# The second layer's messages by units of two chunks, on VectorE alone, in a four-layer graph kernel

## The reference, cut to what matters

```
es = ys[dst]; ev = yv[dst]
m0a = wA * es * sh0
m0b = wD * jnp.einsum('eud,ed->eu', ev, sh1) * INV_SQRT3
m1a = wB[:, :, None] * es[:, :, None] * sh1[:, None, :]
m1b = wC[:, :, None] * ev * sh0[:, :, None]
mid_s = jnp.concatenate([m0a, m0b], axis=1)
mid_v = jnp.concatenate([m1a, m1b], axis=1)
ns = jax.ops.segment_sum(mid_s, src, num_segments=N)
nv = jax.ops.segment_sum(mid_v, src, num_segments=N)
```

## Time and profile before

| | |
|---|---|
| median of 3 runs | 10667.19 us |
| profiled execution | 10687.69 us, span 10685.9 us, mean granted TensorE clock 0.813 |
| DVE busy over the span | 5953.1 us (56%) |
| POOL busy over the span | 5768.1 us (54%) |
| PE busy over the span | 6312.3 us (59%) |
| third stage, first product of DVE to last addition | 5806.15 to 7104.76 us |

### The profile page before, as it was taken

One profiled execution on the slowest core, in us unless ns is written; L12 is line 12 of the kernel. 1 busy time (PEld: TensorE's weight loads), 2 busy tenths in 40 slices (PEclk: granted clock), 3 DMA queues, 4 the chain that ended last, 5 costly groups with the idle time before them and its releaser, 6 DMA issues. The chain is left out here.

```text
span 10685.9 us, 108870 instructions
## 1 busy us (share of the span) xinstructions
PE 6312.3 (59%) x23693; PEld 3434.3 (32%) x23693; DVE 5953.1 (56%) x17820; ACT 2842.7 (27%) x9327; POOL 5768.1 (54%) x6086
## 2 busy tenths in 40 slices
PE   2211344446865666666667777765555578856665
PEld 1101233334433333433334111233333333333332
DVE  8915533430016666544445999976656589943333
ACT  0000000105862222100003777762222236500000
POOL 5776566561006666566662888844555510046664
PEclk9999855558987877888887999996666679978877
DMA  2000111113553333433332555534666645523333
GB/s 79 6 6 5 36 42 46 44 33 124 176 194 96 93 93 93 109 91 91 91 90 67 168 171 169 171 91 141 189 184 186 185 128 176 153 80 91 92 91 82
DMA packets 782920, 1136.72 MB, mean 106 GB/s; under 512 B 161213, under 2 KB 631923, under 8 KB 775629
## 3 DMA queue, kind: packets, MB, share of 16 engines
q0 software_dynamic: 246400, 552.44, 19.6%
q1 hardware_dynamic: 535885, 577.31, 16.6%
HBM read 872.21 MB, written 257.00 MB: 106 GB/s over the span
## 5 line engine op out<-in xcount | busy, mean ns | idle before, releaser
L1155 POOL DMA_INDIRECT ring<-scaled_table,idx_s x832 | 787.2, 946 | 1181.1 <-DVEq L192 773.7
L1029 POOL DMA_INDIRECT big<-x_table,rec_d_sb x808 | 806.1, 998 | 1101.1 <-DMA x_table<-big 726.0
L1748 POOL DMA_INDIRECT ring<-att_table,rec_d_sb x808 | 775.6, 960 | 750.7 <-DVE acc L1858 287.6
L1427 PE MATMUL bank<-ring,wts 128*128 128x512 f32 x1664 | 937.6, 648 | 397.2 <-issue 166.7
L1105 PE MATMUL bank<-iota 128*128 128x512 bf16 x2448 | 1090.0, 445 | 0.0
L333 POOL DMA_INDIRECT rec_s<-acc,big x784 | 837.6, 1068 | 375.0 <-issue 253.7
L1349 POOL DMA_INDIRECT ring<-y_table,idx_s x832 | 815.2, 980 | 395.5 <-DVEq L192 171.3
L333 POOL DMA_INDIRECT rec_d<-x_res,big x784 | 750.5, 957 | 502.0 <-DVE big L596 255.5
L1155 POOL DMA_INDIRECT ring<-h_table,rec_d_sb x808 | 764.1, 946 | 470.6 <-issue 180.4
L1116 PE MATMUL bank<-big,ring 128*128 128x256 f32 x1616 | 620.5, 473 | 501.0 <-issue 363.7
L2088 PE MATMUL bank<-ring 128*128 128x256 f32 x1664 | 644.9, 475 | 421.0 <-DVE ring L2070 244.4
(11 more groups left out here) (344 smaller groups left out, 13324.4 us busy)
## 6 DMA issues: line engine op xcount, KB each, us to landing
weights_dram<-acc SPq DMA_DIRECT2D x104, 1024.0 KB, 4.5
ring<-weights_dram SPq DMA_DIRECT2D x832, 128.0 KB
rows_spill<-ring SPq DMA_DIRECT2D x808, 128.0 KB
big<-rows_spill SPq DMA_DIRECT2D x808, 128.0 KB, 2.2
ring<-key_dram SPq DMA_DIRECT2D x49, 1024.0 KB
big<-dl_dram SPq DMA_DIRECT2D x50, 512.0 KB
ring<-y_table,idx_s POOLq DMA_INDIRECT x832
ring<-scaled_table,idx_s POOLq DMA_INDIRECT x832
```

Source lines behind the costliest of these rows:

```text
L1029: g.indirect_dma_start(out=xg[:, c % RG, :], out_offset=None, in_=x_table, in_offset=bass.IndirectOffsetOnAxis(ap=recd3i[:, c, D_IDX:D_IDX ...
L1155: g.indirect_dma_start(out=slot[:, c % ring_len, :], out_offset=None, in_=table, in_offset=bass.IndirectOffsetOnAxis(ap=index(c), axis=0)) ...
L1427: pe.matmul(ps[6 + u % 2], oh1[c // 4 % 2][:, c % 4, :], mid[:, c % 2, 0:512], start=(c % GS == 0), stop=(c % GS == GS - 1)).then_inc(summ ...
L1748: g.indirect_dma_start(out=ag[:, n % R3, :], out_offset=None, in_=att_table, in_offset=bass.IndirectOffsetOnAxis(ap=recd3i[:, n, D_IDX:D_I ...
```

## The change

DVE's loop goes over units. One instruction takes both chunks of a unit: the reduction (L1391 of the new code), the A and B products together (L1396), the C product (L1399), and, for the unit before, the D product (L1407) and the product with the harmonics (L1410). Then comes the addition (L1420), now of the unit six back (before, a unit was added one chunk after its last product). POOL only gathers. SP loads both chunks' weights by one transfer. ACT makes four one-hot matrices in a row, two units ahead. PE's two products of a unit stand behind one set of waits.

The harmonics (`sh`, 3 floats for an edge) are copied out of the records in `y_vector`, first apart into `ring` and then over the records in `big`. The rest of `big` is then free, and the rings are longer: 16 gathered chunks, 16 chunks of weights, 8 of `mid` and of `dots`, 4 sets of one-hot matrices (two before), and all 8 PSUM banks (two before). The elements computed and the bytes moved stay as they were.

```diff
+        sh, sh_apart = cut(big, 0, NCS * 3, NCS, 3), cut(ring, 1024, NCS * 3, NCS, 3)
...
+            drained(v.tensor_copy(sh_apart, recs3[:, :, S_SH + 1:S_SH + 4]))
+            drained(v.tensor_copy(sh, sh_apart))
...
-        RY = 7
-        yg = cut(ring, 0, RY * (MUL + D), RY, MUL + D)
-        mid = cut(ring, o, 2 * 576, 2, 576)
-        dots = cut(ring, o, 2 * 192, 2, 192)
-        W1 = 8
-        oh1 = [cut(wts, 1408 + 512 * k, 512, 4, P) for k in range(2)]
+        RY, W1, RP = 16, 16, 4
+        o = NCS * 3
+        yg = cut(big, o, RY * (MUL + D), RY, MUL + D)
+        mid = cut(big, o, RP * 2 * 576, RP * 2, 576)
+        oh1 = [cut(wts, 1408 + 512 * k, 512, 4, P) for k in range(2)] + [cut(big, o + 512 * k, 512, 4, P) for k in range(2)]
+        w_rows = cut(ring, 0, W1 * D, W1, D)
+        dots = cut(ring, W1 * D, RP * 384, RP * 2, 192)
+        w_rows_in = slots("w_rows_in", W1 // 2)
...
-            for c in range(NCS):
-                if c >= W1:
-                    sp.wait_ge(mixed.s, c - W1 + 1)
-                sp.dma_start(w_rows[:, c % W1, :], weights_dram[c]).then_inc(w_rows_in.s(c, W1), 16)
-
+            for u in range(NUS):
+                if u >= W1 // 2:
+                    sp.wait_ge(mids_v.s, u - W1 // 2 + 1)
+                sp.dma_start(w_rows[:, 2 * u % W1:2 * u % W1 + 2, :], weights_dram[2 * u:2 * u + 2]
+                             .rearrange("c p k -> p c k")).then_inc(w_rows_in.s(u, W1 // 2), 16)
...
         def third_pool():
...
-                    if n >= RY:
-                        g.wait_ge(mixed.s, n - RY + 1)
...
-                c = n - 6
-                if c >= 0 and c % 2:
-                    g.wait_ge(dotted.s, c + 1)
-                    if c >= 2:
-                        g.wait_ge(summed.s, summed.n(c - 1))
-                    vector_part(g, c).then_inc(mids_g.s, 1)
+            for n in range(NCS):
+                if n >= RY and n % 2 == 0:
+                    g.wait_ge(mids_v.s, (n - RY) // 2 + 1)
...
         def third_scalar():
             a.wait_ge(keys_kept.s, 1)
+            def four_hots(i):
+                hot = oh1[i % 4]
+                if i >= 4:
+                    a.wait_ge(summed.s, summed.n(2 * i - 6))
+                for k in range(4):
+                    ins = a.activation(hot[:, k, :], iota, ACT.Abs, bias=neg_sl[:, 4 * i + k:4 * i + k + 1])
+                then_a(ins)
+                a.activation(hot, hot, ACT.Relu, bias=1.0, scale=-1.0).then_inc(hot_made.s, 1)
+
+            four_hots(0)
+            for u in range(NUS):
+                if u % 2 == 0 and u // 2 + 1 < NCS // 4:
+                    four_hots(u // 2 + 1)
+                for c in (2 * u, 2 * u + 1):
                     y = yg[:, c % RY, MUL:]
                     a.wait_ge(gathered.s(c, RY), gathered.n(c, RY))
-                    if c >= 2:
-                        a.wait_ge(reduced.s, c - 1)
+                    if c % 2 == 0 and u >= RP:
+                        a.wait_ge(reduced.s, u - RP + 1)
                     for d in range(3):
...
+                        ins = a.mul(dots[:, c % (2 * RP), d * MUL:(d + 1) * MUL], y[:, (1 + d) * MUL:(2 + d) * MUL],
+                                    sh[:, c, d:d + 1])
+                ins.then_inc(scaled_y.s, 1)
...
         def third_vector():
             then_v(v.memset(acc, 0.0))
             blk = Numbers(v, regs_v, blk_s_row, NB - 1)
-            for n in range(NCS + 3):
+            LAG = 6
...
+            for n in range(NUS + LAG):
+                u = n
+                if u < NUS:
+                    w4 = of_pair(w_rows, u, W1).rearrange("p c (s u) -> p c s u", s=4)
+                    slot, m = of_pair(yg, u, RY), of_pair(mid, u, 2 * RP)
+                    ends = m[:, :, 384:576].rearrange("p c (s u) -> p c s u", s=3)
+                    vec = m[:, :, 0:384].rearrange("p c (d s u) -> p c d s u", d=3, s=2)
+                    v.wait_ge(scaled_y.s, u + 1)
+                    v.tensor_reduce(slot[:, :, 0:MUL], of_pair(dots, u, 2 * RP).rearrange("p c (d u) -> p c u d", d=3),
...
+                    v.wait_ge(w_rows_in.s(u, W1 // 2), w_rows_in.n(u, W1 // 2))
+                    if u >= RP:
+                        v.wait_ge(summed.s, summed.n(u - RP + 1))
+                    v.tensor_tensor(ends[:, :, 0::2, :], w4[:, :, 0::3, :],
+                                    slot[:, :, MUL:2 * MUL].rearrange("p c (o u) -> p c o u", o=1)
+                                    .to_broadcast([P, 2, 2, MUL]), ALU.mult).then_inc(mixed.s, 1)
+                    v.tensor_tensor(vec[:, :, :, 1, :], w4[:, :, 1:2, :].to_broadcast([P, 2, 3, MUL]),
+                                    slot[:, :, 2 * MUL:].rearrange("p c (d u) -> p c d u", d=3), ALU.mult)
+                u = n - 1
+                if 0 <= u < NUS:
...
+                    v.wait_ge(reduced.s, u + 1)
+                    v.tensor_tensor(m[:, :, 448:512], w4[:, :, 2, :], slot[:, :, 0:MUL], ALU.mult)
+                    v.wait_ge(mixed.s, u + 1)
+
+                    v.tensor_tensor(vec[:, :, :, 0, :], m[:, :, 512:576].rearrange("p c (o u) -> p c o u", o=1)
+                                    .to_broadcast([P, 2, 3, MUL]),
+                                    sh[:, 2 * u:2 * u + 2, :].rearrange("p c (d o) -> p c d o", o=1)
+                                    .to_broadcast([P, 2, 3, MUL]), ALU.mult).then_inc(mids_v.s, 1)
+                u = n - LAG
+                if u >= 0:
+                    v.wait_ge(summed.s, summed.n(u + 1))
...
-                    v.tensor_tensor(here, here, ps[6 + u % 2], ALU.add).then_inc(added.s, 1)
+                    v.tensor_tensor(here, here, ps[u % 8], ALU.add).then_inc(added.s, 1)
...
         def third_tensor():
-            for c in range(NCS):
...
-                pe.wait_ge(mixed.s, c + 1)
-                pe.wait_ge(hot_made.s, hot_made.n(c // 4 + 1))
-                if c % GS == 0 and u >= 2:
-                    pe.wait_ge(added.s, added.n(u - 1))
-                pe.matmul(ps[6 + u % 2], oh1[c // 4 % 2][:, c % 4, :], mid[:, c % 2, 0:512],
-                          start=(c % GS == 0), stop=(c % GS == GS - 1)).then_inc(summed.s, 1)
+            for u in range(NUS):
+                pe.wait_ge(mids_v.s, u + 1)
+                if u % 2 == 0:
+                    pe.wait_ge(hot_made.s, hot_made.n(u // 2 + 1))
+                if u >= 8:
+                    pe.wait_ge(added.s, added.n(u - 7))
+                for c in (2 * u, 2 * u + 1):
+                    ins = pe.matmul(ps[u % 8], oh1[c // 4 % 4][:, c % 4, :], mid[:, c % (2 * RP), 0:512],
+                                    start=(c % 2 == 0), stop=(c % 2 == 1))
+                ins.then_inc(summed.s, 1)
```

More of the change, by code:

```diff
@@ L1360, in third_scalar @@
+        def third_pool():
+            for n in range(NCS):
+                if n >= RY and n % 2 == 0:
+                    g.wait_ge(mids_v.s, (n - RY) // 2 + 1)
+                g.indirect_dma_start(
+                    out=yg[:, n % RY, MUL:], out_offset=None, in_=y_table,
+                    in_offset=bass.IndirectOffsetOnAxis(ap=idx_s[:, n:n + 1], axis=0)
+                ).then_inc(gathered.s(n, RY), 16)
         def third_scalar():
             a.wait_ge(keys_kept.s, 1)
-            for n in range(NCS + 7):
-                c = n - 7
-                if c >= 0:
+            def four_hots(i):
[11 more added lines that the diff above has]
+                for c in (2 * u, 2 * u + 1):
```

74 lines of the change are left out of this document (12 added, 62 removed).

## The result

The changed kernel took 10749.33 us (median of 6 runs, 10720.28 to 10786.37) where the kernel before took 10671.29 us (6 runs, 10621.88 to 10686.57): a ratio of 1.010, 95% interval 1.007 to 1.013. It is 1.0% slower; the forecast was 1.8% faster. The profiled run took 10783.69 us, 96 more than that of before (10687.69). Its third stage, from the first vector product to the start of the last addition, goes from 5777.1 to 7209.6 us: 1432.5 us instead of 1298.6.

A forecast was written before the change was run, and what follows sets the result against it. Third stage bound by POOL and by DVE with its PE wait, about 2.94 us a unit. 5806 + 1092 + 2 = 6900 instead of 7105, less 10: gain 195, forecast 10472 us; own range 10430 to 10520, 8-in-10 range to 10590.

The forecast's parts named there:

- DVE's unit: Third stage: six DVE instructions a unit take 2.56 us, from start distances; with block-number loads 1092 us for 416 units.
- the 27 us for the loads of block numbers: Third stage, DVE: 26 loads of block numbers stay and each counts in full, 1.04 us each, 27 us.
- The low end of the forecast's own range: Whole time 10430 us, if POOL takes 2.50 us a unit and nothing else is in the way.
- PE: Third stage: PE's four records take 2.23 us a unit at full clock, so it waits for DVE.
- the wait for it: Third stage: DVE's 0.26 us wait a unit for PE's product goes, since `mid` holds four units.
- the copies: Two harmonics copies, 5.4 us together, run while `y_table` lands in 10.9 us, so they cost nothing.
- the ends: Third stage: first product still starts at 5806.15 us; at the end about 2 us remain, as before.
- POOL: Third stage: two gathers take 2.50 to 2.58 us a unit, 1040 to 1073 us, just below DVE, costing nothing.
- ACT: Third stage: same instructions, at most 1016 us or 2.44 a unit; four one-hots in a row stay covered, two units ahead.
- The first rival: Third stage: gathers set the pace at 1.44 us a chunk, stage 1198 us, total 10568 us; chance 0.12.
- The clock rival: Third stage: TensorE loses its clock; at 0.75 the stage takes 1389 us, total 10757 us; chance 0.04.
- No overlap on the new forms: Third stage: each new DVE instruction occupies its full duration, 3.00 us a unit, total 10645 us; chance 0.06.

The follow-up runs named there:

- without gathers: Changed kernel with only the first 16 of the third stage's 832 gathers issued, later units using old rows again: 10409.08 us on a slower chip.
- ring of twelve: Changed kernel with DVE's addition moved between the C and D products and 12 gathered chunks instead of 16: ratio 0.976 on a faster chip, 0.9985 on a slower.
- the addition between: Changed kernel with DVE's addition moved from the unit's end to between the C and D products, 16 gathered chunks kept: 10617.10 us on a slower chip.
- ring of eight: Changed kernel with 8 gathered chunks instead of 16 and nothing else: 10556.93 us on a slower chip.

## Why the prediction was wrong

*DVE's unit: right, its stage in part by luck.* 2.57 us against 2.56. With twelve places the stage is 1090 us against 1092 + 2, but the 27 us for the loads of block numbers are not in it: in the changed kernel DVE's waits before the addition L1420 sum to 1.1 us, and without gathers the stage takes 1072.5, about 416 x 2.57. The rest up to 1090 is 17.2 us in which DVE waits for ACT. (The 1088 us above are some 13 too long as an estimate of DVE's own work: idle time is counted from a record's end, and at full pace the reduction starts 0.08 us before that, in 162 places.) The low end of the forecast's own range does not follow from its sum either: with DVE at 1092 us a POOL at 2.50 us a unit does not shorten the stage.

*PE, the wait for it, the copies, the ends: right.* In the changed kernel DVE's waits for PE sum to under 1 us, and with a ring of twelve on a faster chip PE is busy for 828 us at a clock of 0.99.

*POOL: the step that failed.* It said that two gathers need 2.50 to 2.58 us a unit, just below DVE, "so such an engine just below the bound costs nothing". The 1.29 and 1.25 came from the earlier trace rows: beside DVE in its old order, and beside a stage with little on DVE. The change lengthened DVE's unbroken run of two-input products from 0.90 us (5830.28 to 5831.18) to 1.47 us, and 181 of 832 gathers then took over 2.1 us. The 288 us of excess of all gathers lengthened the stage by about 145 on a slower chip. The prediction listed POOL's slowing of DVE but never asked what DVE does to POOL. In before the shorter runs held no gather over 1.1 us: the one at 5830.53 in the earlier trace rows starts 0.25 us into a run and takes 0.98. In the changed kernel none that starts outside a run is caught, on either chip (with the addition between there are a few, 5 of 727 in the slower chip's run with a ring of twelve); why 88 of the 393 that start inside one in the changed kernel still take under 1.1 us, no run here settles.

*ACT: the second step that failed.* "I see nothing that removes it", of the cover of the one-hots. The cover held against work and did not hold against 20 spells in which ACT stood still. The first rival had the signs of them, 1.44 us a chunk in two stages with waits for nothing visible, and was given 0.12, with 96 us of the gain lost. Its argument against itself, "two gathers landed for each unit here without ACT or DVE running short", rested on a kernel whose gathers a product interrupts: before's longest row of gathers no more than 1.5 us apart is 7, the changed kernel's 24. The size was off too, since it priced a longer pitch of gathers and not a standstill of ACT: the spells cost 176 to 194 us. What in the chip makes them stays open.

*The clock rival.* The clock did fall, from 0.98 to 0.88, but it is not what lengthened the stage: DVE's waits for PE sum to under 1 us, and where the spells are gone the clock is 0.99, on a slower chip (ring of eight) as on a faster one. That this rival's 10757 us lies 8 us from the measured 10749 is chance.

*No overlap on the new forms:* refuted by the starts above, 0.46 us apart at 0.55 each. The section of the Trainium skill that the prediction cites for it (VectorE: DVE Perf Modes, The DRAIN you can't avoid) adds that an instruction that is not held starts earlier, so it leaves room for what both traces show.

So the mechanism of the gain was there and of about the right size: 195 us were forecast, and a ring of twelve with the addition between gives 221 us on a faster chip (173 on a slower one without gathers, which leaves out work). What failed was to take an engine at 95 to 98% of the bound, whose duration hangs on its neighbour, for free.

## What to carry to other kernels

Where GpSimd issues indirect gathers, look at how long DVE's unbroken runs of instructions with two SBUF inputs are after the change, and put one that reads PSUM between them: the same six instructions in another order were worth 144 to 166 us. How deep gathers may run ahead has a best length that differs between chips: of those tried with that order, twelve is the best where ACT has no such spells, and eight where it has (one run). And time a change on more than one chip when its gain hangs on a dense stream of gathers.

## What the hardware showed that was not expected

The same kernel takes 10582 to 10671 us on some chips and 9007 to 9053 on two others. Whether that belongs to the chip, or to something that ran beside the kernel there, no run here tells; one chip was faster in both of its turns. The difference begins in code that this change does not touch. In the preparation, line 448 issues 784 small matmuls while GpSimd issues indirect transfers that write rows (L333, 1.27 us apart). Its row and its wait in before, on a slower chip, with three of its records:

```profile
L448 PE MATMUL bank<-big x784: 176/329/542, 1221.3 to 2382.2; 128*128 128x400 bf16 x49, 128*128 128x300 bf16 x49, 128*128 128x200 bf16 x49, 128*128 128x100 bf16 x49
...
  issue: 244.5, 152
...
1262.70 0.22 PE L448 MATMUL bank<-big 128*128 128x75 bf16 x1 [1.20 <-issue]
1264.11 0.20 PE L448 MATMUL bank<-big 128*128 128x50 bf16 x1 [1.19 <-issue]
1265.53 0.18 PE L448 MATMUL bank<-big 128*128 128x25 bf16 x1 [1.21 <-issue]
```

and the same line of the version with a ring of twelve, on a faster chip, where it has no idle row at all:

```profile
L448 PE MATMUL bank<-big x784: 176/308/542, 820.5 to 1301.1; 128*128 128x400 bf16 x49, 128*128 128x300 bf16 x49, 128*128 128x200 bf16 x49, 128*128 128x100 bf16 x49
```

The 784 matmuls take 1161 us from first to last on the slower chip and 481 on the faster. The 1.41 and 1.42 us between starts are close to those of ACT in the spell above (1.39 to 1.41). On the slower chips, while GpSimd issues indirect transfers 1.25 to 1.27 us apart, other engines fall into spells of one instruction per 1.4 us. Two such distances (1.37 to 1.45 us) in a row stand on PE 23 to 37 times and on DVE 78 to 131 times in each of the ten traces of slower chips; in the ten of faster ones there are none on PE and at most one on DVE. A gather-only stage of 808 chunks shows the same: 1157 to 1169 us on a slower chip and 1014 us, 1.25 a chunk, on a faster one. What in the chip does it, no run here shows.
